# Start of a graph network kernel: w_hh turned ahead of the first input, later loads asked for behind half of the first adjacency, the third input loaded ahead of a second adjacency in halves

## The reference

```
A = (adj != 0)
h = x
for l in range(5):
    m   = h @ weight[l]
    agg = einsum('bij,bid->bjd', A, m)
    h   = gru_cell(agg, h, w_ih, w_hh, b_ih, b_hh)
x = layernorm(x + h * mask)
# second part: five small graph convolutions over the first 25 nodes of each graph,
# relu, weighted sum, residual, layernorm
x = layernorm(x + gnn(x, adj, W1, b1, W2, b2, fusion_w))
```

## Time and profile before

| | |
|---|---|
| median of 3 runs | 493.06 us (493.0 to 493.22) |
| profiled execution | 493.06 us, of which the span of its instructions is 491.3 us |
| TensorE matmul busy | 480.5 us (98%) |
| VectorE, ScalarE, GpSimd busy | 352.4 us (72%), 303.6 us (62%), 334.5 us (68%) |
| DMA | 55.72 MB, mean 113 GB/s |
| granted TensorE clock, 27 to 461.8 us | 1.00 |

### The profile page before, as it was taken

The page is one execution under the profiler, slowest core; times in us unless marked ns, Lnnn a source line. Parts: engine busy times, 40 slices in busy tenths (PEclk is TensorE's granted clock), DMA queues, the critical chain, the costliest instruction groups (busy, mean ns, idle before and its releaser), DMA issues.

```text
span 491.3 us, 7178 instructions
## 1 busy us (share of the span) xinstructions
PE 480.5 (98%) x2301; PEld 229.6 (47%) x2301; DVE 352.4 (72%) x659; ACT 303.6 (62%) x537; POOL 334.5 (68%) x378
## 2 busy tenths in 40 slices
PE   7999999999999999999999999999999999999994
PEld 5444444444444444444444444444444444564554
DVE  3777867696867687778587777877668675445796
ACT  4556655655655656776657775576765776655564
POOL 3654774748775698997689748659996776334466
PEclk9999999999999999999999999999999999999998
DMA  8878252565535537264955476323443233322313
GB/s 271 258 172 157 45 150 54 151 155 140 120 63 151 118 88 184 57 142 107 175 112 163 106 211 166 73 43 77 89 106 83 57 65 63 65 43 42 83 45 86
DMA packets 133676, 55.72 MB, mean 113 GB/s; under 512 B 97297, under 2 KB 125414, under 8 KB 133638
## 3 DMA queue, kind: packets, MB, share of 16 engines
q1 hardware_dynamic: 108356, 32.39, 32.1%
q10 hardware_dynamic: 25282, 22.87, 14.9%
HBM read 27.46 MB, written 4.19 MB: 64 GB/s over the span
## 4 chain that ended last, share of the span: by engine, by line
PE 83%; POOL 6%; DVE 3%; DMA 3%; ACT 2%; issue 2%; POOLq 0%; DVEq 0%; ACTq 0%
PE pA L790 24%; PE pR L795 6%; PE pR L797 6%; PE pR L796 6%; PE pZ L797 6%; PE pZ L796 6%; PE pZ L795 6%; PE pIN L795 3%; PE pHN L795 3%; PE pHN L796 3%; PE pHN L797 3%; PE pIN L797 3%; PE pIN L796 3%; POOL ZH L528 2%; POOL HT L539 1%
## 5 line engine op out<-in xcount | busy, mean ns | idle before, releaser
L539 POOL TENSOR_TENSOR HT<-H,HT 128x512 f16<-128x512 f32 x76 | 91.8, 1208 | 90.1 <-ACT HT L1167 90.1
L790 PE MATMUL pA<-A,NAT 128*128 128x512 fp8e4 x640 | 151.0, 379 | 0.0
L528 POOL TENSOR_TENSOR ZH<-Z,H 128x512 f32<-128x512 f32 (+1 forms) x80 | 102.6, 1283 | 28.7 <-ACT Z L1182 27.2
L1422 DVE SCALAR_TENSOR_TENSOR T<-pHN,BHN,R 128x512 f32<-128x512 f32 (+1 forms) x80 | 59.9, 749 | 78.2 <-ACT R L1174 77.8
L1187 ACT ACTIVATE pIN<-T,COLS 128x512 f32<-128x512 f32 (+1 forms) x80 | 55.2, 691 | 71.1 <-DVE T L1426 71.0
L790 PEld LDWEIGHTS pA<-A,NAT 128*128 128x128 f16 x640 | 62.5, 98 | 74.8 <-issue 1.0
L1167 ACT ACTIVATE HT<-H 128x512 f16<-128x512 f32 x76 | 47.8, 628 | 64.8 <-DVE H L1436 64.6
L1432 DVE SCALAR_TENSOR_TENSOR pIN<-Z,pIN 128x512 f32<-128x512 f32 (+1 forms) x80 | 55.1, 689 | 24.4 <-ACT pIN L1187 24.2
L1174 ACT ACTIVATE R<-pR,BRZ 128x512 f32<-128x512 f32 (+1 forms) x80 | 54.3, 679 | 20.1 <-PE pR L797 19.4
L1436 DVE TENSOR_TENSOR H<-ZH,pIN 128x512 f32<-128x512 f32 (+1 forms) x80 | 54.8, 685 | 10.1 <-POOL ZH L528 7.7
L1416 DVE TENSOR_TENSOR AG<-pA,AG 128x512 f16<-128x512 f32 x80 | 54.7, 684 | 7.7 <-ACT AG L1163 7.7
(11 more groups left out here) (284 smaller groups left out, 810.1 us busy)
## 6 DMA issues: line engine op xcount, KB each, us to landing
AS<-in_adj_dram ACTq DMA_DIRECT2D x13, 1024.0 KB, 5.9
XR<-in_x_dram ACTq DMA_DIRECT2D x16, 256.0 KB, 2.9
XS<-in_x_dram ACTq DMA_DIRECT2D x13, 256.0 KB, 3.3
out_dram<-Y SPq DMA_DIRECT2D x16, 192.0 KB, 2.2
AS<-in_adj_dram SPq DMA_DIRECT2D x2, 1024.0 KB, 8.7
AS<-in_adj_dram SPq DMA_DIRECT2D x4, 256.0 KB, 5.4
NAT<-HT SPq DMA_TRANSPOSE x64, 3.2
XS<-in_x_dram SPq DMA_DIRECT2D x3, 256.0 KB, 7.8
```

The lines of the kernel that those rows point to most:

```text
L528: g_.tensor_tensor(ZH[:, cs], Z[:, cs], H[:, b, cs], ALU.mult).then_inc(zh_p, 1)
L539: g_.tensor_tensor(HT[:, b, 1, :], H[:, b, :], HT[:, b, 0, :], ALU.subtract).then_inc(h_lo, 1)
L790: last = mm(pA2[:, k % 2, :], NAT[:, k % 2, h, i, :], A8[:, b, i, :], start=(h == 0 and i == 0), stop=(h == 1 and i == NI - 1))
L1422: v.scalar_tensor_tensor(out=T[:, cs], in0=pHN[:, cs], scalar=BHN[:, 0:1], in1=R[:, cs], op0=ALU.add, op1=ALU.mult).then_inc(t_v, 1)
```

## The change

Seven places are touched. TensorE transposes `w_hh` before it transposes the first input. Its first products take the low half of `WH` before the low half of `HT`. ScalarE and VectorE split `WH` before `HT` of graph 0; ScalarE's `natural_hi(0)` moves behind the copy of `WT`, and `natural_hi(2)` from behind the update gate of step 0 to ahead of its reset gate. GpSimd's `natural_lo(2)` moves ahead of `kept_share(0)`. SyncE's wait behind the first adjacency is for that adjacency's second block instead of `w_ih`; behind it x of graph 2 goes ahead of adjacency 1, which is issued in two halves with a semaphore each, so that `cast_half(1, 0)` waits for its own half.

```diff
@@ sync
-            sp.wait_ge(ld_wi, 32)
+            sp.wait_ge(ld_a0[1], 16)
             load_x(1)
-            load_a(1)
             load_x(2)
+            for h in range(2):
+                sp.dma_start(AS[:, 1, 2 * h:2 * h + 2, :],
+                             adj[1, 2 * h * P:2 * h * P + 2 * P, :].rearrange("(i p) n -> p i n", p=P))\
+                    .then_inc([ld_a1_0, ld_a[1]][h], 16)
             load_a(2)
             load_x(3)
@@ gpsimd
             natural_lo(1)
+            natural_lo(2)
             kept_share(0)
-            natural_lo(2)
             first_state(1)
@@ tensor, first_gates_of_state
                 for bank, g in banks:
                     mm(bank[:, :], WH[:, 0, g, :], hi, start=True, stop=False)
+                pe.wait_ge(wh_lo, 1)
+                for bank, g in banks:
+                    mm(bank[:, :], WH[:, 1, g, :], hi, start=False, stop=False)
                 pe.wait_ge(x_lo, 1)
                 for bank, g in banks:
-                    mm(bank[:, :], WH[:, 0, g, :], lo, start=False, stop=False)
-                pe.wait_ge(wh_lo, 1)
-                for bank, g in banks:
-                    mm(bank[:, :], WH[:, 1, g, :], hi, start=False, stop=(bank is pHN))
+                    mm(bank[:, :], WH[:, 0, g, :], lo, start=False, stop=(bank is pHN))
@@ tensor
-            transpose_x(0, pF)
             pe.wait_ge(ld_wh, 16)
             for g in range(3):
                 last = tr(pA2[:, 1, g * D:(g + 1) * D], WHS[:, g, :], IDF[:, :])
             last.then_inc(wh_t, 1)
+            transpose_x(0, pF)
             pe.wait_ge(ld_wi, 32)
@@ scalar
-            natural_hi(0)
-            transposed_hi(0, pF)
             act.wait_ge(wh_t, 1)
             fn(WH[:, 0, :, :].rearrange("p g d -> p (g d)"), pA2[:, 1, 0:3 * D], ACT.Copy,
                scale=WSCALE).then_inc(wh_hi, 1)
+            transposed_hi(0, pF)
             act.wait_ge(wi_t, 1)
             fn(WT, pIN[:, :], ACT.Copy).then_inc(wi_v, 1)
+            natural_hi(0)
             merged_hi(0, pIN)
             natural_hi(1)
             aggregated_hi(0)
             transposed_hi(1, pF)
+            natural_hi(2)
             act.wait_ge(cols_v, 1)
             reset_gate(0)
             update_gate(0)
-            natural_hi(2)
             new_gate(0)
@@ vector, cast_half
-                dve.wait_ge(ld_a[b % 3], 16 * (b // 3 + (b % 3 > 0)))
+                if b == 1 and h == 0:
+                    dve.wait_ge(ld_a1_0, 16)
+                else:
+                    dve.wait_ge(ld_a[b % 3], 16 * (b // 3 + (b % 3 > 0)))
@@ vector
-            transposed_lo(0, pF)
             dve.wait_ge(wh_hi, 1)
             split_lo(WH[:, 0, :, :], WH[:, 1, :, :], pA2[:, 1, :]).then_inc(wh_lo, 1)
+            transposed_lo(0, pF)
             cast_first(0)
```

More of the change, by code:

```diff
@@ L278, in graph_net_kernel @@
         ld_a = [sem(f"ld_a{i}") for i in range(3)]
+        ld_a1_0 = sem("ld_a1_0")
         ld_a0 = [sem(f"ld_a0_{i}") for i in range(NI)]
```

## The result

The changed kernel took 495.29 us in the median of 5 runs, the kernel before 493.0: a ratio of 1.0049 (1.0037 to 1.0061). Forecast were 493.3 us and a range of 492.3 to 494.5, with a chance of 0.84 for no difference of over 0.2% and of 0.12 for slower, which is what came. The median loss is 2.3 us. Lines have moved by 4 to 7: L794, L799, L1417, L1423, L1429 here are L790, L795, L1410, L1416, L1422 of the kernel before.

What follows compares the result with a forecast made beforehand. TensorE's own work was taken to bound the middle, so shifts at the start pass to the end one for one. +0.75 us up to step 1's messages and -0.47 at step 2 gave +0.28, 493.3 us, range 492.3 to 494.5.

Steps and rivals of the forecast that it cites:

- First hole: TensorE's 0.40 us idle before the first state product: product starts 0.37 us earlier, 0.16 left at step 0's aggregation.
- The wait in SyncE's queue: SyncE's later wait: x 1 lands at 11.1 instead of 10.35, step 0's messages start 0.35 us late.
- The third input ahead: x 2 loaded before adjacency 1, its low half on GpSimd delaying a cast: step 1's messages start 0.75 us late.
- landing of adjacency 1: In SyncE's queue, behind x 2: the halves land at about 13.5 and 15.1 us, both at 13.6 before.
- casts: Step 1's two casts on VectorE: `natural_lo(2)` holds the first, `T` starts 0.75 us later, 0.40 of it new.
- Third hole: TensorE's 0.47 us idle before step 2's state product, waiting for x 2's DMA transpose: gone, transpose landed by 22.3.
- Sum: Whole kernel: +0.75 us up to step 1's messages, -0.47 at step 2, together +0.28 us, 493.3 us.
- Rival 1: x 1 lands early, at 10.7, and step 1's cast is free: -0.5 us, 492.3 to 492.6; chance 0.28.
- The slower rival: x 1 lands late, at 12.45, making step 0's messages 1.70 late: +1.6 us in all, 494.7; chance 0.10.
- Rival 3: x 2's transpose is not sooner, idle before step 2's state product stays: +0.75 us, 493.8; chance 0.12.
- Rival 4: Clock falls to 1.2 GHz after TensorE idles before step 0's messages: 2.2 us more, 495.5; chance 0.05 with the rest.

Runs made afterwards that it cites:

- second trace: The changed kernel run again with no edit, for another trace: 495.22 us median, ratio 1.0031 to the kernel before.

## Why the prediction was wrong

- *First hole.* Right: 6.80 for 6.94, and the aggregation at 9.05 for 9.2 (9.57 in the second trace). The casts of adjacency 0 were pushed back as I had allowed (0.54 us of idle time inside the aggregation), and it was hidden by ScalarE's wait for x 1, as I had taken.
- *The wait in SyncE's queue.* Right for x 1: landed at 10.98 for 11.1, `AG` at 11.69 for 11.64, messages at 13.16 for 13.11. In the second trace x 1 was as early, but the messages came at 13.71, held by the blocked addition, which I had not counted.
- *The third input ahead.* This step failed, in two terms.
  The **landing of adjacency 1**: forecast 13.5 and 15.1 with a bound of 15.4, measured 15.63 and 16.91. I had taken the 3.2 us between two landings of the kernel before as the price of 1 MB and laid them behind the new landing of x 1. Measured, the transfer takes 7.4 us from its issue before and 7.8 after, and its issue moved from 6.18 to 9.07. The 3.2 us were small because x 1 had itself been held up to 10.35. With the issue at 9.07 plus 7.4 I would have written 16.5. The late wait is most of the delay and x 2 the rest: with x 2 ahead and the wait as before the last half landed at 14.0 to 14.6, with x 2 behind it at 13.15, with the late wait at 16.3 to 16.9. The emptier queue gave none of it back: the engines moved 289 GB/s where they had moved 346, and part of that was for later loads. Why they slow down between 11 and 12 us, and why some parts come 1 to 3 us behind the first, is not shown.
  The **casts**: forecast 0.40 us for one collision, measured 1.9 (3.20 for 1.28). I had looked only for the operation that the change moves, and not for what GpSimd does next: the share of step 0 starts at 15.5, so a pair of casts, 1.28 us, that begins later than about 14.2 meets it. Before, it had ended 0.2 us ahead (14.89 for 15.08).
  A smaller slip in the same step: I had `HT` high of graph 1 right behind `AG`, at 12.13, though it waits for TensorE's transposes (12.37 in the kernel before). It came at 12.78, so `natural_lo(2)` ran from 13.97 for 13.3, and VectorE was ready for the casts at 14.09 for 13.45. Even with the data early that left them next to GpSimd's operations, as the kernel with the wait as before shows.
- *Third hole.* Right that it is gone, and the transpose landed at 22.23 for 22.3. In part this is luck: in the second trace it landed at 23.5, behind the 23.39 at which I had TensorE ask for it, and was in time only because TensorE was over 2 us late.
- *Sum.* +0.75 up to step 1's messages should have been +3.89 in this trace (+2.89 in the second). Less the 0.47 of the third hole that is 3.4 and 2.4, and the spans grew by 3.6 and 2.7.
- *Rivals.* Rival 1 fell: the casts were not free. The slower rival had the wrong place: x 1 was on time, the adjacency was late. Its size (+1.6, measured +2.3) was near by accident. Rival 3 fell in the first trace (22.23), and in neither did TensorE wait for the transpose. Rival 4 fell: the granted clock was 1.00 (2.4 GHz) in the stretch around the 2.18 us of idle time and in all that follow, up to 470 us.
- The rule on the ports (the Trainium skill, SBUF — State Buffer, Who interferes with whom) was the one that spoke against the change, and it counted twice where I had let it count once. The estimate for x 1 by the Trainium skill (DMA: Bandwidth & Descriptors, Anatomy of one DMA) was close (2.6 for 2.9); it says nothing of 7.3 us for 512 KB behind 512 KB.

## What to carry to other kernels

When a load is asked for later, price its landing by the issue-to-landing time of that same transfer, not by the distance between two landings. Then look at everything the other engine of a shared port does behind the slot in which an operation ran undisturbed: a slip past the edge of that slot costs whole operations of the other engine (2 us here for casts of 1.3), and holding the other engine back with a wait can win that back (1.7 to 2.0 us here). It only helps where the data are there: with the late load the same wait gained nothing (496.04).

## What the runs showed of the hardware

- A waiting cast is let in between two GpSimd operations that stand back to back, and the second of these is then the one that waits: in the changed kernel L521 took 1.60 us from 16.70, 1.15 when undisturbed. So two casts alternate with GpSimd's operations, and a pair that is caught with both costs two of them: 3.20, 3.33 and 3.33 us in three kernels, where a pair alone takes 1.28.
- Size doesn't protect: the addition of 128x2 (L1671, both inputs in `COLS`) took 1.17 us in one trace and 0.94 in another under GpSimd's L511, 0.16 without it. The low half of `AG` (L1423, one input in the bank `pA`) took 0.69 us at 12.32 in the changed kernel though L511 ran from 11.71 to 12.86.
- The DMA transpose of x 2 (256 KB) took 3.1 us where adjacency 3 was asked for later and little else was in the queues, and 3.9 to 8.3 us in the other traces; being issued 0.47 us ahead of adjacency 3 was not enough (issued at 17.18 against 17.65, it took 6.4 us).
- The kernel before, run again beside each group, has a tail: 29 executions in one group from 492.29 to 495.26 us, with a median of 493.33. The casts' narrow slot would explain it; no run shows that.
